# Both attentions of a two-layer block on one core: the loops over batches written out

## The chip, the cores and the metric

The kernel runs on one core of a Trainium2 chip. Five engines take part: TensorE (PE, with its weight loads PEld), VectorE (DVE), ScalarE (ACT), GpSimd (POOL) and SyncE (SP, which here only issues DMAs). The metric is the device time of one execution in microseconds (us).

## The reference

The input x is 8 batches of 512 tokens of 128 features, float32. Four stages follow each other, and each adds to x:

```python
x = x + attn_a(layernorm(x))   # 16 heads of 8, q and k normalised to length 1, softmax(g * q.k)
x = x + ffn(layernorm(x))      # router, top 2 of 8 experts, at most 384 tokens per expert
x = x + attn_b(layernorm(x))   # 16 heads of 64, position bias, softmax, output projection
x = x + ffn(layernorm(x))      # the same weights of the experts again
```

## The kernel before

Five blocks run one after the other: a short setup, attention a (about 20 to 500 us of the profile), the experts, attention b (about 610 to 1680 us), the experts again. In each block every engine has its own program, and the engines meet through semaphores that only count up. A step waits for a count that grows with the batch: `wait(eng, signal, b, k)` (L71) waits for `base + b * per + k`.

In both attentions a batch is software-pipelined into the next one: while batch b is worked on, its successor is normalised and projected, and the router's steps of its predecessor are done. Batch 0 has no predecessor and batch 7 no successor, so these two are written out in Python with constants. Batches 1 to 6 are one loop of the hardware on each engine, in which b is a register: the body stands once in the program, each wait whose count depends on b is computed in registers (`REGISTER_ALU` in the order of instructions), addresses in x_res are computed too, and each of the engines ends the body with its own compare-and-branch. No engine waits for the others at the end of a body. There are five jumps back for six passes, on each engine, in each attention.

What the steps of the prediction name:

- Attention a, per batch 32 chunks: PE makes scores (L836) in one of two PSUM buffers, ACT makes exponentials (L620), PE multiplies them with v (L850), DVE takes the sum over (`take`, L714) and normalises it (`finish`, L719 to L726). DVE's chain of small steps for the lengths of q and k is L660 to L682. At chunk 31 PE makes the router's counts (L301, L303), which wait for DVE (L256). PE's branch is at L899.
- Attention b, per batch 16 steps: PE makes scores (L1232), DVE adds the bias and takes the minimum (`lowest`, L1422), ACT makes exponentials (L1351), PE turns them (L1243), ACT and DVE copy the turned half each (L1343, L1430), PE multiplies with v (L1257), DVE scales (`finish`, L1443, which writes ctxT). At the last step PE makes the output projection (L1267) and DVE adds it to x (`residual`, L1448). DVE's branch is at L1507, ACT's at L1387, PE's at L1310.
- Below, "the seam" of a batch in attention b is the place right after the residual of the batch before it, which is also where DVE's loop jumps back.

The Python condition in attention a's `prepare` on PE (`if not isinstance(b, int) or b > 2`) and the two forms of the operands at stage 0 on DVE depend on whether b is a register.

Of the kernel before, what the change touches and what calls it, by code (L numbers as in the profile page):

```python
# [21 lines left out]
B, S, D = 8, 512, 128  # L22
# [40 lines left out]
def prime(eng):  # L63

    while Signal.made:
        eng.sem_inc(Signal.made.pop().sem, Signal.BASE)


def wait(eng, signal, b, k):

    eng.wait_ge(signal.sem, signal.at(b, k))  # L71
# [327 lines left out]
def attention_a(nc, g, sem):  # L399
# [5 lines left out]
    with ctx:  # L405
# [76 lines left out]
        @block.sync  # L482
        def _(sp):
            prime(sp)
            for n, name in enumerate(("a_Wq", "a_Wk", "a_Wv")):
                sp.dma_start(w_raw[:, n, :], g[name]).then_inc(w_in, 16)
            sp.dma_start(gs[:, :], g["g_scale"].to_broadcast([P, 1])).then_inc(gs_in, 16)
            sp.wait_ge(clear_a, 3)

            def parts_to_dram(b):  # L490

                wait(sp, lo_ready, b, 1)
                for n in range(3):
                    sp.dma_start(k_dram[n].rearrange("d h t -> h d t"), parts[:, n, 1, :]).then_inc(parts_out.sem, 16)
                for n in range(5):
                    sp.dma_start(q_dram[n].rearrange("d h t -> h d t"), parts[:, n % 3, 0, :]).then_inc(parts_out.sem, 16)
                wait(sp, parts_out, b, 16 * 8)
                sp.sem_inc(g["passed_sp"], 1)

            def stacks(grp):  # L500

                r, heads = 3 * DA, slice(4 * grp, 4 * grp + 4)
                for m in range(3):
                    sp.dma_start(k_stack[m * r:(m + 1) * r, heads, :],
                                 k_dram[:, :, heads, :].rearrange("n d h t -> (n d) h t")).then_inc(stacks_in[grp].sem, 16)
                    sp.dma_start(q_stack[m * r:(m + 1) * r, heads, :],
                                 q_dram[m:m + 3, :, heads, :].rearrange("n d h t -> (n d) h t")).then_inc(stacks_in[grp].sem, 16)

            def clears(b):

                sp.dma_start(g["bias_skew"][:, bass.ds(b * (P // B), P // B), :],
                             g["rows"][:, :].unsqueeze(1).to_broadcast([HEADS, P // B, REL])).then_inc(cleared, 16)
                blank(1, b, cleared)

            def blank(f, n, done):
                sp.dma_start(g["slots"][f][bass.ds(n * CAP, CAP), :].rearrange("(p r) w -> p (r w)", p=P),
                             g["blank"][:, :, :].rearrange("p r w -> p (r w)")).then_inc(done, 16)

            def store_x(b):
                wait(sp, res_done, b, GROUPS)  # L520
                sp.sem_inc(g["passed_sp"], 1)
                sp.dma_start(g["x_mid"].rearrange("(b t p) d -> b p t d", b=B, p=P)[bass.ds(b, 1), :, :, :].rearrange("o p t d -> (o p) t d"),
                             x_res[:, bass.ds(b * TB, TB), :]).then_inc(x_stored, 16)

            def batch(b, before):
                for grp in range(GROUPS):
                    wait(sp, stacks_in[grp], b, 16 * 6)
                    sp.sem_inc(g["passed_sp"], 1)
                if before:
                    store_x(b - 1)  # L530
                parts_to_dram(b + 1)
                for grp in range(GROUPS):
                    wait(sp, s_ready, b, 8 * grp + 8)
                    stacks(grp)
                clears(b)

            r.load(sp)
            parts_to_dram(0)
            for grp in range(GROUPS):
                stacks(grp)  # L540
            batch(0, False)
            for n in range(B):
                blank(0, n, slots_clear)
            with sp.Fori(1, B - 1) as b:
                batch(b, True)
            clears(B - 1)
            store_x(B - 2)
            store_x(B - 1)
            sp.wait_ge(cleared, 16 * 2 * B)
            sp.wait_ge(x_stored, 16 * B)  # L550

        @block.gpsimd
        def _(pool):
            nc.gpsimd.memset(q_stack[64:P, :, :], 0.0).then_inc(clear_a, 1)
            nc.gpsimd.memset(k_stack[64:P, :, :], 0.0).then_inc(clear_a, 1)
            pool.wait_ge(clear_a, 2)
            nc.gpsimd.memset(v_ext[:, :, :, :], 0.0).then_inc(clear_a, 1)
            pool.wait_ge(clear_a, 3)
            nc.gpsimd.memset(v_ext[:, :, :, DA:DA + 1], 1.0).then_inc(clear_a, 1)
            pool.wait_ge(clear_a, 4)  # L560

            
            def move_v(grp):
                heads = slice(4 * grp, 4 * grp + 4)
                nc.gpsimd.tensor_copy(v_ext[:, :, heads, 0:DA], v_stage[:, :, heads, :]).then_inc(v_ready.sem, 1)

            def inverse_std(lo, hi, n):
                pool.wait_ge(ln_var, n)
                nc.gpsimd.tensor_tensor(rstd[:, lo:hi], var[:, lo:hi], g["neg_half"][:, 0:hi - lo],
                                        ALU.pow).then_inc(ln_rstd, 1)  # L570

            def batch(b, before):
                if before:
                    r.inverse_std(pool, b - 1)
                wait(pool, v_staged, b + 1, 1)
                for grp in range(GROUPS):
                    wait(pool, av_done, b, 2 * grp + 2)
                    pool.sem_inc(g["passed_pool"], 1)
                    move_v(grp)
                    if before and grp == 0:  # L580
                        r.copy_rows(pool, b - 1)
                if before:
                    r.scatter(pool, b - 1)

            inverse_std(0, TB, 1)
            r.constants(pool)
            wait(pool, v_staged, 0, 1)
            for grp in range(GROUPS):
                move_v(grp)
            inverse_std(TB, NT, 2)  # L590
            batch(0, False)
            pool.wait_ge(slots_clear, 16 * B)
            with pool.Fori(1, B - 1) as b:
                batch(b, True)
            for b in (B - 2, B - 1):
                r.inverse_std(pool, b)
                r.copy_rows(pool, b)
                r.scatter(pool, b)

        @block.scalar  # L600
        def _(act):
# [24 lines left out]

            square(0)
            attend(0, False, True)
            with act.Fori(1, B - 1) as b:
                attend(b, True, True)  # L630
            attend(B - 1, True, False)
            r.exps(act, B - 1)
# [2 lines left out]
        def _(dve):  # L635
# [136 lines left out]
            dve.wait_ge(r.const, 4)  # L772
            dve.wait_ge(ln_rstd, 2)
            batch(0, False, True)
            with dve.Fori(1, B - 1) as b:
                batch(b, True, True)
            batch(B - 1, True, False)
            take(B - 1, 3)
# [11 lines left out]
        def _(pe):  # L790
# [105 lines left out]
                prepare(0, stage)  # L896
            pe.wait_ge(r.w_in, 16)
            attend(0, False, True)
            with pe.Fori(1, B - 1) as b:  # L899
                attend(b, True, True)  # L900
            attend(B - 1, True, False)
            for n in range(2):
# [133 lines left out]
def attention_b(nc, g, sem):  # L1036
    ctx = ExitStack()
    with ctx:
# [84 lines left out]
        def _(sp):  # L1123
# [34 lines left out]

            inverse_rows(0, 0)
            batch(0, False, True)  # L1160
            with sp.Fori(1, B - 1) as b:
                batch(b, True, True)
            batch(B - 1, True, False)
            store_x(B - 1)
# [2 lines left out]
        @block.gpsimd  # L1167
        def _(pool):
            for n in two:
                nc.gpsimd.memset(inv_pad[n][:, :], 0.0).then_inc(pad_clear, 1)  # L1170
            def batch(b, before, more):
                if before:
                    r.inverse_std(pool, b - 1)
                    r.copy_rows(pool, b - 1)
                    r.scatter(pool, b - 1)
                if more:
                    norm_pool(nc, pool, g, ln, lnb, b + 1)

            norm_pool(nc, pool, g, ln, lnb, 0)
            r.constants(pool)  # L1180
            batch(0, False, True)
            with pool.Fori(1, B - 1) as b:
                batch(b, True, True)
            batch(B - 1, True, False)
            r.inverse_std(pool, B - 1)
            r.copy_rows(pool, B - 1)
            r.scatter(pool, B - 1)

        @block.tensor
        def _(pe):  # L1190
# [116 lines left out]

            for d in range(LEAD, LAST):
                step(0, d, d >= FIRST)
            with pe.Fori(1, B - 1) as b:  # L1310
                for d in range(FIRST, LAST):
                    step(b, d, True, b - 1)
            for d in range(FIRST, LAST):
# [6 lines left out]
        def _(act):  # L1320
# [63 lines left out]

            for d in range(LEAD, LAST):
                step(0, d, d >= FIRST)
            with act.Fori(1, B - 1) as b:  # L1387
                for d in range(FIRST, LAST):
                    step(b, d, True, b - 1)
            for d in range(FIRST, LAST):  # L1390
# [4 lines left out]
        def _(dve):  # L1395
# [108 lines left out]
            dve.wait_ge(x_in[1], 16)  # L1504
            for d in range(FIRST, LAST):
                step(0, d, True)
            with dve.Fori(1, B - 1) as b:  # L1507
                for d in range(FIRST, LAST):
                    step(b, d, True, b - 1)
            for d in range(FIRST, LAST):  # L1510
# [84 lines left out]
```

## Time and profile before

| | us |
|---|---|
| three executions | 1774.84 median, 1772.44 to 1777.78 |
| the profiled execution | 1776.62 |
| its span, first to last instruction | 1774.9 |
| share of the span: PE, ACT, DVE, POOL busy | 81%, 53%, 50%, 15% |
| instructions in the profile | 27286 |

The profile shows, for a core's engines, when each instruction ran and, where an engine sat idle before one, what released it. An instruction of a register, a wait or a branch is not counted as busy. "issue" as the releaser means that the engine waited for nothing that the profile shows. A row of the timeline gives start, duration, engine, line, operation and, in brackets, the idle time before it and its releaser. A row of windows gives a stretch, its length, the busy time of PE, PEld, DVE, ACT and POOL with the number of instructions (of DVE alone where it says so), the granted TensorE clock (1.00 is 2.4 GHz, 0.50 would be 1.2 GHz throughout), the DMA share and GB/s.

### The profile page before, as it was taken

The page shows a single profiled execution, that of the slowest core. Times are in us where ns is not written, and L with a number is a line of the kernel's source. Part 1 is how long each engine was busy: PE and PEld are TensorE (multiplying, and loading weights), DVE is VectorE, ACT ScalarE, POOL GpSimd, SP SyncE. Part 2 cuts the span into 40 slices and gives each one's busy share as a digit, 9 for nine tenths or more (in the row PEclk, how much of TensorE's full clock was granted, in tenths as well). Part 3 has the DMA queues.
Part 4 walks back from the last instruction along what each step waited for, and adds up shares of the span by engine and source line. Part 5 has one row for each costly group of instructions (what it writes and reads, how often), then busy time and mean ns, then how long its engine had stood idle before and what let it go on. Part 6 is the DMA issues. An engine that isn't in the chain of part 4 may idle for free. (4 is left out here: it accounts for less than half of the span.)

```text
span 1774.9 us, 27286 instructions
## 1 busy us (share of the span) xinstructions
PE 1444.2 (81%) x7697; PEld 718.2 (40%) x7735; DVE 889.2 (50%) x2700; ACT 936.4 (53%) x1844; POOL 269.3 (15%) x277
## 2 busy tenths in 40 slices
PE   2388788877629089999999998998998998999464
PEld 1122222222217034454454454554544544544343
DVE  2445545444311036657656666557566566566311
ACT  0367666667404047656655655655656565565031
POOL 4101122222124400001001002002002002001135
PEclk9999998999859579999999999999999999999777
DMA  3355444555229300001001000000000000000052
GB/s 67 78 104 134 91 97 89 112 111 110 36 75 287 60 12 19 21 17 33 24 14 36 19 24 24 18 25 20 19 19 18 19 24 13 18 25 19 13 142 25
DMA packets 83135, 93.73 MB, mean 53 GB/s; under 512 B 19934, under 2 KB 60845, under 8 KB 83024
## 3 DMA queue, kind: packets, MB, share of 16 engines
q1 hardware_dynamic: 72016, 86.21, 19.5%
q0 software_dynamic: 11008, 6.39, 2.6%
q14 instruction: 84, 0.69, 0.1%
q8 instruction: 27, 0.44, 0.1%
HBM read 61.75 MB, written 36.09 MB: 55 GB/s over the span
## 5 line engine op out<-in xcount | busy, mean ns | idle before, releaser
L1422 DVE CUSTOM_DVE_ANT_0 biased<-s_ps,bias 128x512 f32<-128x512 f32 x512 | 332.8, 687 | 98.7 <-PE s_ps L1232 60.5
L1351 ACT ACTIVATE probs_b<-biased,low 128x512 f32<-128x512 f32 x512 | 362.7, 711 | 17.3 <-DVE low L1422 17.3
L620 ACT ACTIVATE probs_a<-score_ps,gbound 128x1024 f32<-128x1024 f32 x256 | 269.1, 1114 | 155.3 <-PE score_ps L836 127.0
L1343 ACT ACTIVATE pT<-p_ps 128x512 f32<-128x512 f32 x256 | 152.3, 595 | 323.5 <-PE p_ps L1243 278.5
L1243 PE MATMUL p_ps<-ident,probs_b 128*128 128x128 f32 x2048 | 281.5, 279 | 39.0 <-ACT pT L1343 22.7
L1243 PEld LDWEIGHTS p_ps<-ident,probs_b 128*128 128x128 f32 x2048 | 229.9, 142 | 203.8 <-issue 124.7
L1232 PE MATMUL s_ps<-kT,qT 64*128 64x512 f32 x1024 | 264.5, 635 | 1.4 <-ACT kT L1337 1.4
L1257 PE MATMUL o_psb<-pT,v_b 128*64 128x512 f32 x1024 | 233.8, 598 | 0.0
L1430 DVE COPY pT<-p_ps 128x512 f32<-128x512 f32 x256 | 176.3, 689 | 54.2 <-PE p_ps L1243 49.5
L836 PE MATMUL score_ps<-q_stack,k_stack 128*128 128x512 bf16 x474 | 140.1, 401 | 58.1 <-ACT probs_a L620 30.0
L330 POOL DMA_INDIRECT slots<-rows_r,slot_r x128 | 126.1, 985 | 363.9 <-DVE slot_r L279 324.6
L1232 PEld LDWEIGHTS s_ps<-kT,qT 64*128 64x128 f32 x1024 | 89.9, 192 | 138.2 <-issue 106.3
L1443 DVE TENSOR_TENSOR ctxT<-o_psb,inv_row 128x512 f32<-128x512 f32 x64 | 44.3, 692 | 198.9 <-PE o_psb L1257 194.5
L850 PE MATMUL o_ps<-probs_a,v_ext 128*32 128x512 f32 x1024 | 142.3, 630 | 0.0
L1257 PEld LDWEIGHTS o_psb<-pT,v_b 128*64 128x64 f32 x1024 | 67.8, 136 | 157.0 <-issue 155.9
L316 POOL TENSOR_TENSOR ln_r_r<-ln_vareps_r,neg_half 128x4 f32<-128x4 f32 x16 | 16.5, 1034 | 593.9 <-DVE ln_vareps_r L212 540.9
L836 PEld LDWEIGHTS score_ps<-q_stack,k_stack 128*128 128x128 bf16 x512 | 41.9, 101 | 150.0 <-ACT probs_a L620 97.4
L1351 ACT ACTIVATION_READ_ACCUMULATOR probs_b<-biased,low 128x1 f32 x512 | 97.6, 191 | 0.0
L714 DVE COPY o_sb<-o_ps 128x512 f32<-128x512 f32 x32 | 22.1, 692 | 150.5 <-PE o_ps L850 141.8
L1015 DVE TENSOR_TENSOR o_b_f<-O_f,e_b 128x384 f32<-128x384 f32 x16 | 8.9, 557 | 134.0 <-PE O_f L989 129.0
L1223 PE MATMUL m_ps<-xT_b,wk 128*128 128x512 f32 x128 | 70.8, 635 | 1.7 <-ACT qT L1337 1.7
L1210 PE MATMUL m_ps<-wv,xT_b 128*128 128x512 f32 x128 | 68.5, 618 | 1.5 <-ACT v_b L1331 0.8
(148 smaller groups left out, 1338.1 us busy)
## 6 DMA issues: line engine op xcount, KB each, us to landing
inv_row<-inv_rows SPq DMA_DIRECT2D x128, 128.0 KB
k_stack<-k_parts SPq DMA_DIRECT2D x96, 96.0 KB
q_stack<-q_parts SPq DMA_DIRECT2D x96, 96.0 KB
bias_skew<-bias_rows SPq DMA_DIRECT2D x8, 1024.0 KB
w_f<-in_w SPq DMA_DIRECT2D x32, 256.0 KB, 5.5
bias<-bias_skew SPq DMA_DIRECT2D x16, 448.0 KB
q_parts<-parts SPq DMA_DIRECT2D x40, 128.0 KB, 2.4
inv_rows<-inv_turned SPq DMA_DIRECT2D x256, 1.0 KB
```

Source lines behind the costliest of these rows:

```text
L330: self.nc.gpsimd.indirect_dma_start(self.g["slots"][self.f], bass.IndirectOffsetOnAxis(ap=self.slot[:, k, t:t + 1], axis=0), self.rows[:, ...
L620: nc.scalar.activation(probs[q % 2][:, c % 4, :], score_ps[c % 2][:, :], ACT.Exp, bias=gbound[:, :]).then_inc(p_ready.sem, 1)
L836: last = nc.tensor.matmul(score_ps[c % 2][:, n * S:(n + 1) * S], k_stack[:, head, kt * P:(kt + 1) * P], q_stack[:, head, :], start=True, s ...
L850: last = nc.tensor.matmul(o_ps[hh * VW:(hh + 1) * VW, :], v_ext[:, half * 2 + n, grp * 4 + hh, :], probs[q % 2][:, hh, n * S:(n + 1) * S], ...
L1223: nc.tensor.matmul(m_ps[:, :], (wq, wk)[part][:, n * P:(n + 1) * P], xT[:, :], start=True, stop=True).then_inc(qk_ps.sem, 1)
L1232: last = nc.tensor.matmul(s_ps[k % 2][s][:, :], qT[n % 2][own(s), i * P:(i + 1) * P], kT[n % 2][own(s), :], start=True, stop=True)
L1243: last = nc.tensor.transpose(p_ps[s][:, i * P:(i + 1) * P], probs[n % 2][:, s, i, kt * P:(kt + 1) * P], g["ident"][:, :])
L1257: last = nc.tensor.matmul(o_ps[own(s), :], v[:, kt, h * DH:(h + 1) * DH], pT[t % TB][s][:, :], start=(kt == 0), stop=(kt == TB - 1), skip_ ...
L1343: nc.scalar.activation(pT[t % TB][0][:, :], p_ps[0][:, :], ACT.Copy).then_inc(pT_ready[0].sem, 1)
L1351: nc.scalar.activation(probs[n % 2][:, s, i, :], biased[k % 2][s][:, :], ACT.Exp, bias=low[n % 2][:, s, i:i + 1], scale=-1.0, accum_out=su ...
L1422: nc.vector.tensor_tensor_reduce(out=biased[k % 2][s][:, :], in0=s_ps[k % 2][s][:, :], in1=bias[:, h, off:off + S], scale=1.0, scalar=3.0e ...
L1430: nc.vector.tensor_copy(pT[t % TB][1][:, :], p_ps[1][:, :]).then_inc(pT_ready[1].sem, 1)
```

## The change

Ten loops of the hardware become Python loops. Each engine's program now holds batches 1 to 6 one after the other, with constants for the counts and addresses, and no branch. The operations on data, their order on each engine, the buffers and the counts waited for stay. One of the ten places, the others alike (SP, POOL, ACT, DVE and PE in attention a; SP, POOL, PE, ACT and DVE in attention b):

```diff
             for d in range(FIRST, LAST):
                 step(0, d, True)
-            with dve.Fori(1, B - 1) as b:
+            for b in range(1, B - 1):
                 for d in range(FIRST, LAST):
                     step(b, d, True, b - 1)
             for d in range(FIRST, LAST):
                 step(B - 1, d, False, B - 2)
```

What DVE's program of attention b held at the end of the loop's body, up to the branch (L1422 is `lowest`, L71 a wait's register arithmetic, L1448 the residual):

```order
L1422 ISA biased,low<-s_ps,bias 128x512 [waits p_ready_b]
L1422 ISA low 128x1
L71 REGISTER_ALU
L1430 COPY pT<-p_ps 128x512 [waits pT_ps,av_done_b]
L1448 ISA [waits y_done_b]
L1448 TENSOR_TENSOR x_res<-x_res,m_ps 128x512
L1507 REGISTER_ALU
L1507 COMPARE_AND_BRANCH
```

and what stands at the same place of batch 1 in the program after the change, with the first rows of batch 2 behind the residual:

```order
L1422 ISA biased,low<-s_ps,bias 128x512 [waits p_ready_b]
L1422 ISA low 128x1
L1430 COPY pT<-p_ps 128x512 [waits pT_ps,av_done_b]
L1448 TENSOR_TENSOR x_res<-x_res,m_ps 128x512 [waits y_done_b]
L1422 ISA biased,low<-s_ps,bias 128x512 [waits p_ready_b,s_ready_b]
L1422 ISA low 128x1
```

The register arithmetic and the branch are gone; the data operations follow each other as before.

On PE at the end of attention a's body (L301 and L303 are the router's counts, L836 the scores) there stood:

```order
L71 REGISTER_ALU
L301 MATMUL aux_ps<-chosen_r,upper 128x32 [waits r_step0]
L303 MATMUL aux_ps<-before_r,ones_sq 128x32
L899 REGISTER_ALU
L899 COMPARE_AND_BRANCH
```

and now, with the first scores of the next batch:

```order
L303 MATMUL aux_ps<-before_r,ones_sq 128x32
L836 MATMUL score_ps<-q_stack,k_stack 128x512 [waits p_ready,stacks_in0]
L836 MATMUL score_ps<-q_stack,k_stack 128x512
L836 MATMUL score_ps<-q_stack,k_stack 128x512 [waits p_ready]
```

The scores stand directly behind the counts. Counted in rows of this order with their repeats, DVE's body of attention b held 407 entries, of which 146 were register arithmetic, and ACT's 263 with 130; attention a's bodies held 156 on DVE and 79 on ACT.

## Rows read from the trace of the kernel before

**Rows 1.** The page's first line.

```profile
span 1774.9 us, 27286 instructions
```

**Rows 2.** Windows: batches 4 and 5 of attention b, seam to seam (us, busy, PEclk).

```profile
1159.25:1288.39 129.14, 123.25 (x646) 64.76 (x646) 80.26 (x241) 76.60 (x186) 10.53 (x11) 0.99 0.07 20
1288.39:1416.20 127.81, 121.85 (x646) 64.02 (x646) 80.18 (x241) 76.60 (x186) 10.55 (x11) 1.00 0.06 19
```

**Rows 3.** Timeline of DVE at a seam inside the loop.

```profile
1159.25 0.69 DVE L1448 TENSOR_TENSOR x_res<-x_res,m_ps 128x512 f32 x1 [5.92 <-PE m_ps L1267]
1162.70 0.69 DVE L1422 CUSTOM_DVE_ANT_0 biased<-s_ps,bias 128x512 f32<-128x512 f32 x1 [2.76 <-issue]
```

**Rows 4.** What is on line L1507, DVE's branch in attention b (ns).

```profile
L1507 DVEq COMPARE_BRANCH  x6: 55/63/74, 900.9 to 1545.3; - x6
```

**Rows 5.** Timeline of DVE behind the seam where the loop is entered, without a jump back.

```profile
774.22 0.69 DVE L1422 CUSTOM_DVE_ANT_0 biased<-s_ps,bias 128x512 f32<-128x512 f32 x1 [0.53 <-PE s_ps L1232]
...
782.21 0.69 DVE L1443 TENSOR_TENSOR ctxT<-o_psb,inv_row 128x512 f32<-128x512 f32 x1 [2.98 <-PE o_psb L1257]
```

**Rows 6.** Windows of DVE: residual to a later ctxT (L1443), batches 1 to 6; 1, 7.

```profile
773.00:782.21 9.21, 5.29 (x15) 1.00 0.01 3
900.83:911.54 10.71, 5.20 (x16) 1.00 0.01 2
1030.21:1040.57 10.36, 5.20 (x15) 1.00 0.01 2
1159.25:1169.82 10.57, 5.20 (x16) 1.00 0.01 2
1288.39:1298.94 10.55, 5.20 (x15) 1.00 0.01 2
1416.20:1426.57 10.37, 5.21 (x16) 1.00 0.01 2
773.00:825.39 52.39, 36.68 (x113) 1.00 0.07 21
1545.25:1598.10 52.85, 36.61 (x113) 1.00 0.08 21
```

**Rows 7.** Timeline of PE at the seam of rows 3.

```profile
1154.80 4.29 PE L1267 MATMUL m_ps<-wo,ctxT 128*128 128x128 f32 x37
...
1164.67 0.66 PE L1243 MATMUL p_ps<-ident,probs_b 128*128 128x128 f32 x4 [1.34 <-DVE pT L1430]
```

**Rows 8.** Timeline of ACT at the same seam.

```profile
1161.63 0.60 ACT L1343 ACTIVATE pT<-p_ps 128x512 f32<-128x512 f32 x1 [7.40 <-PE p_ps L1243]
```

**Rows 9.** Timeline of PE at a batch's end in attention a.

```profile
217.25 0.41 PE L301 MATMUL aux_ps<-chosen_r,upper 128*128 128x32 f32 x2 [0.97 <-DVE before_r L256]
```

**Rows 10.** Timeline of ACT: first exponentials of batches 3 and 7, attention a.

```profile
218.55 1.11 ACT L620 ACTIVATE probs_a<-score_ps,gbound 128x1024 f32<-128x1024 f32 x1 [1.91 <-PE score_ps L836]
...
426.73 1.11 ACT L620 ACTIVATE probs_a<-score_ps,gbound 128x1024 f32<-128x1024 f32 x1 [1.71 <-PE score_ps L836]
```

**Rows 11.** What is on line L899, PE's branch in attention a (ns).

```profile
L899 PEldq COMPARE_BRANCH  x6: 76/215/238, 166.0 to 425.7; - x6
```

**Rows 12.** Windows of DVE: L660 to L682 for batch 1 (constants) and 4 (registers).

```profile
88.37:94.72 6.35, 5.91 (x17) 1.00 0.00 0
240.86:247.21 6.35, 5.91 (x17) 1.00 0.00 0
```

**Rows 13.** Windows: batches 4 and 6 of attention a, first exponentials to the next.

```profile
270.38:324.47 54.09, 44.35 (x249) 15.22 (x252) 26.51 (x85) 34.54 (x35) 10.72 (x14) 0.91 0.47 99
376.19:426.73 50.54, 40.33 (x248) 14.33 (x252) 26.35 (x84) 34.40 (x35) 10.69 (x14) 1.00 0.46 96
```

**Rows 14.** Timeline of ACT in batch 3 of attention a.

```profile
235.43 1.11 ACT L620 ACTIVATE probs_a<-score_ps,gbound 128x1024 f32<-128x1024 f32 x1 [4.89 <-remote]
```

**Rows 15.** The page's DMA queues that carry instructions: packets, MB, share.

```profile
q14 instruction: 84, 0.69, 0.1%
q8 instruction: 27, 0.44, 0.1%
```

More of the change, by code:

```diff
@@ L543, in _ @@
                 blank(0, n, slots_clear)
-            with sp.Fori(1, B - 1) as b:
+            for b in range(1, B - 1):
                 batch(b, True)
@@ L592, in _ @@
             pool.wait_ge(slots_clear, 16 * B)
-            with pool.Fori(1, B - 1) as b:
+            for b in range(1, B - 1):
                 batch(b, True)
@@ L628, in _ @@
             attend(0, False, True)
-            with act.Fori(1, B - 1) as b:
+            for b in range(1, B - 1):
                 attend(b, True, True)
@@ L774, in _ @@
             batch(0, False, True)
-            with dve.Fori(1, B - 1) as b:
+            for b in range(1, B - 1):
                 batch(b, True, True)
@@ L898, in _ @@
             attend(0, False, True)
-            with pe.Fori(1, B - 1) as b:
+            for b in range(1, B - 1):
                 attend(b, True, True)
@@ L1160, in _ @@
             batch(0, False, True)
-            with sp.Fori(1, B - 1) as b:
+            for b in range(1, B - 1):
                 batch(b, True, True)
@@ L1181, in _ @@
             batch(0, False, True)
-            with pool.Fori(1, B - 1) as b:
+            for b in range(1, B - 1):
                 batch(b, True, True)
@@ L1309, in _ @@
                 step(0, d, d >= FIRST)
-            with pe.Fori(1, B - 1) as b:
+            for b in range(1, B - 1):
                 for d in range(FIRST, LAST):
@@ L1386, in _ @@
                 step(0, d, d >= FIRST)
-            with act.Fori(1, B - 1) as b:
+            for b in range(1, B - 1):
                 for d in range(FIRST, LAST):
@@ L1506, in _ @@
                 step(0, d, True)
-            with dve.Fori(1, B - 1) as b:
+            for b in range(1, B - 1):
                 for d in range(FIRST, LAST):
```

## The prediction

> **What bounds the kernel now.** I looked for the seams between batches first, because the change acts there and on the register arithmetic inside a batch, and nowhere else. The windows of whole batches give attention b's rhythm: 129.14 us for a batch, in which PE is busy 123.25 and DVE 80.26 [rows 2]. So PE sets attention b's pace, and a delay on another engine counts only as far as PE comes to wait for it. Then the timeline at the seam: behind the residual DVE stands idle for 2.76 us although no semaphore holds it ("issue") [rows 3]. The branch itself takes 63 ns by its record [rows 4]; what follows it takes the time. Where the loop is entered without a jump back, the same `lowest` starts after 0.53 us and its wait is for PE [rows 5]. PE has meanwhile begun the next scores, and then waits 1.34 us for DVE's copy of the turned half [rows 7]. That is the stall arriving on the engine that sets the pace.
>
> In attention a the batch takes 50.54 to 54.09 us with PE busy 40 to 44 [rows 13]: PE, ACT and DVE wait for one another in turn, so a latency anywhere in that ring can count.
>
> **The change part by part.**
>
> *DVE's jumps back in attention b.* I measure what one costs to the end of the kernel, not what DVE idles. From the residual to the first ctxT behind it the batch takes 9.21 us in the pass that was entered from above, and 10.71, 10.36, 10.57, 10.55 and 10.37 in the five passes entered by a jump [rows 6]. They sum to 52.56; five times 9.21 is 46.05; the jumps cost 6.51 us together, 1.30 each. The rest of the 2.76 is taken up by slack that DVE has there. With the stall gone, `lowest` waits for PE's scores again, as in [rows 5]. The upper bound of a seam is its whole idle time less that wait, 2.76 - 0.53 = 2.2, so 11 for five; the shift of ctxT is nearer to the time of the batch, since PE's work of that batch follows it, and I take 6.5.
>
> Here a page bears on it. The Trainium skill, "Runtime: NRT & Kernel Launch", section "Instruction fetch mechanics", says that a taken branch whose target isn't in the two pages at hand forces a fetch of the page before execution goes on. The trace agrees: the large body of DVE (407 entries) stalls by microseconds, the small ones of attention a don't. The skill's "Advanced Engine Details and Errata", section "Control Flow Timing", gives about 108 ns for a compare-and-branch; by that alone five jumps would be an estimated 0.5 us and nobody could measure the change. Rows 3 decide for the larger cost.
>
> *ACT's jump in attention b.* Its copy after the seam had stood idle 7.40 us waiting for PE [rows 8], so whatever the jump costs lies in that wait: 0. If the cover were gone it could cost what DVE's does.
>
> *PE's jump in attention b.* It is issued while the output projection of 4.29 us runs [rows 7]: 0.
>
> *PE's jump in attention a.* The counts wait for DVE and start at 217.25 [rows 9]; the scores of the next batch stand behind them and the branch, and ACT waits for these scores: 1.91 us at a jump, and 1.71 where batch 7 is entered and the branch falls through [rows 10]. The branch takes 215 ns in the middle and 76 at least [rows 11], which agrees. Five times 0.20 is 1.0 us. Bounds: 0, if the loading of k and q ends last there after the change, and 5 x 0.24 = 1.2, the longest record.
>
> *Other jumps.* DVE in attention a jumps while waiting for PE's last values, SP while its transfers run, POOL behind its scatter and ahead of work for which nobody is yet waiting. I take 0 for them together. An unhidden jump would be at most PE's 0.24 each time, since none of these short bodies shows an idle stretch like that of rows 3.
>
> *Register arithmetic.* DVE's seventeen small dependent steps are where it should show: 6.35 us with constants, for batch 1, and 6.35 with registers, for batch 4 [rows 12]. It runs ahead of the engine's work. Over a longer stretch I compare pass 1 with batch 7, which was written out already and does the same up to there: 52.39 with registers, 52.85 with constants [rows 6]. So constants gain nothing; I take 0, with 0.46 a batch as the bound on the loss side (6 x 0.46 = 2.8 us). On the gain side ACT's 1.91 against 1.71 is the only such difference, and it is booked above already; I allow the same 0.20 once more per batch in attention a, 1.2 us.
>
> *Fetching more code.* The program's instruction packets on one queue are few, 27 [rows 15], so most of one engine's passes fetched nothing. Now every batch's code comes from memory once. Pass 1 and batch 7 ran code for the first time, at 52.39 and 52.85 us, no slower than the others less their jump. I take 0.
>
> **The sum.** 6.5 + 1.0 = 7.5 us. The profiled execution took 1776.62 us, its span 1774.9 [rows 1], the 1.7 outside it stays. It becomes 1769.1. That execution lies 1.8 above the median of the three, so on the median's scale 1774.84 - 7.5 = 1767.3 us, a gain of 0.42%. A change of less than 0.3% (5.3 us) is about what a measurement of this kernel can't tell from none.
>
> **The rivals.**
>
> *The clock and the ring move.* PE's granted clock was 0.99 in one batch of attention b and 1.00 in the next, and the batches took 129.14 and 127.81 [rows 2]; both had their jump, so 1.3 us a batch hang on whether PE drops to 1.2 GHz for a short while after a pause. In attention a ACT once waits 4.89 us for something that the profile doesn't name [rows 14], and equal batches differ by 3.55 us [rows 13]. The change shifts all phases. Should three batches more or fewer fall into the slow kind in attention b and one in attention a, that is 3 x 1.3 + 3.5 = 7.4: the gain is eaten, 1775 us, or doubled, 1760. For it: this is as large as the spread of the three executions, 5.3 us. Against: five of six passes behave alike, so the pattern is stable. Chance 0.20 towards no change, 0.06 towards a double gain.
>
> *Another wait takes the stall's place.* DVE's stall also lets PE's scores pile up; without it PE may run into ACT's copies or the transfers of the softmax sums. Pass 1 and batch 7 speak against it: their first ctxT still comes early and the lead of 1.4 us is kept to the fourth. If two thirds were given back, 2.2 + 1.0 would remain: 1771.6 us. Chance 0.08.
>
> *Slower: the written-out code comes late.* One mechanism: an engine that reaches code not yet fetched waits as DVE did behind its branch, 2.76 us, of which 1.3 reach the end. Before, the small bodies of attention a and PE's body of attention b were kept; now they are fetched anew each batch, in attention a beside transfers that keep the DMA engines 46% busy [rows 13]. Two late pieces a batch in twelve batches are 24 x 1.3 = 31 us, less 7.5: 1798 us. It decides from 6 late pieces on (no gain), and from 10 on it is slower by more than 0.3%. Against it stand the first passes above. Chance 0.08.
>
> That the change does nothing at all is excluded by the order: the branches are gone.
>
> **How the numbers follow.** Forecast 0.58, of its own range 1763 to 1770; moved phases 0.20 against me and 0.06 for me; stall replaced 0.08; late code 0.08. The predicted time is the forecast's. The range from 1761 to 1775 takes in the forecast with its bounds (gain 7.5 + 1.2 + 1.3 for a batch without the slow clock, or 7.5 - 2.8) and the moved phases, and leaves out late code and the far end of a double gain, some 0.15. Faster by over 0.3%: the forecast except its lower tenth (0.52), the double gain (0.06) and a part of the moved phases (0.09), 0.67. Within 0.3%: what is left of those and the replaced stall, 0.24. Slower: 0.09.
>
> **What would show each step.** In the changed kernel's profile: at all seven seams of attention b the first `lowest` follows the residual after a wait for PE of about 0.5 us and no "issue" of 2 us or more; residual to ctxT is 9.2 to 9.3 us in every batch; a batch is 127.8 us, or 126.5 where the clock stays up; ACT's wait at the start of batches 2 to 6 of attention a is 1.71 instead of 1.91; the chain L660 to L682 stays at 6.35; the instruction packets rise in number without an idle stretch at "issue" beside them. The prediction is wrong if ctxT comes early but the batch is as long as before, if batches of attention a move by more than their seams, or if new idle stretches of 2 to 3 us at "issue" appear inside a batch.

## The result, and the profile after

The changed kernel takes 1758.28 us (median of 7 runs, 1757.22 to 1772.67); the kernel before, beside it, 1772.44 (7 runs, 1770.03 to 1777.78). The ratio is 0.993, with an interval of 0.991 to 0.9951: 12.4 us less by the ratio, 14.2 between the medians. The forecast was a gain of 7.5, to 1767.3 us, with a range from 1761. The direction is right, the size too small, and the time lies below the range.

The profiled execution happens to be the slowest of the seven, 1772.67 us, so I read its seams, not its total. First the page's own lines, which answer to [rows 1, 15]:

```profile
span 1771.0 us, 23821 instructions
...
q8 instruction: 63, 1.03, 0.2%
q14 instruction: 58, 0.48, 0.1%
```

There are 3465 fewer instructions, no branch, and 1.51 MB of instruction packets where there were 1.13. Then DVE's timeline at the same seam as [rows 3]:

```profile
1156.02 0.69 DVE L1448 TENSOR_TENSOR x_res<-x_res,m_ps 128x512 f32<-128x512 f32 x1 [6.01 <-PE m_ps L1267]
1157.23 0.69 DVE L1422 CUSTOM_DVE_ANT_0 biased<-s_ps,bias 128x512 f32<-128x512 f32 x1 [0.52 <-PE s_ps L1232]
```

The idle 2.76 us at "issue" are gone, and `lowest` waits 0.52 us for PE, as it did at the entry [rows 5]. DVE's windows from the residual to the ctxT behind it, answering to [rows 6] (the first is batch 1, the last three are batches 4 to 6):

```profile
773.28:782.65 9.37, 5.29 (x15) 1.00 0.00 0
...
1156.02:1165.40 9.38, 5.29 (x16) 1.00 0.00 1
1284.89:1294.27 9.38, 5.29 (x16) 1.00 0.00 0
1412.55:1422.09 9.54, 5.29 (x15) 1.00 0.00 1
```

10.36 to 10.71 became 9.37 to 9.54. The five middle passes add up to 47.05 us where they had 52.56, so 1.10 a seam (0.83 to 1.33 each), a little under the 1.30 of the forecast, and the entry case itself went from 9.21 to 9.37. Whole batches 4 to 6 of attention b, against [rows 2]:

```profile
1156.02:1284.89 128.87, 124.89 (x646) 65.55 (x647) 80.43 (x242) 76.75 (x186) 10.54 (x11) 0.97 0.07 20
1284.89:1412.55 127.66, 123.64 (x646) 65.28 (x647) 80.42 (x242) 76.75 (x186) 10.51 (x11) 0.99 0.07 20
1412.55:1538.80 126.25, 122.21 (x646) 64.13 (x646) 80.14 (x241) 76.63 (x186) 10.51 (x11) 1.00 0.07 20
```

Identical work takes 126.25 or 128.87 us, beside a granted clock of 1.00 or 0.97. DVE's chain of L660 to L682 takes 6.36 us in batch 3 (6.35 in [rows 12]). The seams account for 5.5 us of a measured 12.4. The profiled execution can't show the rest: its stretch of attention a, from the first exponential of batch 0 to that of batch 7, takes 355.0 us, no less than the 354.2 before. So I took the change apart.

### The profile page after: what moved, and what is told of

It reads as the page before. It is cut to its first block and busy times, and to the rows that moved or that the text cites. A ratio compares the mean times of both kernels' runs of the same rounds, so it can differ in the third digit from the quotient of the medians.

```text
span 1771.0 us, 23821 instructions
## 1 busy us (share of the span) xinstructions
PE 1463.2 (83%) x7735; PEld 722.8 (41%) x7735; DVE 888.3 (50%) x2700; ACT 937.3 (53%) x1844; POOL 269.1 (15%) x277
## 5 line engine op out<-in xcount | busy, mean ns | idle before, releaser
L1422 DVE CUSTOM_DVE_ANT_0 biased<-s_ps,bias 128x512 f32<-128x512 f32 x512 | 332.6, 688 | 74.9 <-PE s_ps L1232 54.9
L1343 ACT ACTIVATE pT<-p_ps 128x512 f32<-128x512 f32 x256 | 152.1, 594 | 325.6 <-PE p_ps L1243 288.4
L836 PE MATMUL score_ps<-q_stack,k_stack 128*128 128x512 bf16 x512 | 151.5, 409 | 47.3 <-ACT probs_a L620 24.0
L330 POOL DMA_INDIRECT slots<-rows_r,slot_r x128 | 125.9, 983 | 364.1 <-DVE slot_r L279 326.3
L850 PE MATMUL o_ps<-probs_a,v_ext 128*32 128x512 f32 x1024 | 146.9, 649 | 0.0
L1443 DVE TENSOR_TENSOR ctxT<-o_psb,inv_row 128x512 f32<-128x512 f32 x64 | 44.3, 692 | 200.4 <-PE o_psb L1257 197.4
L836 PEld LDWEIGHTS score_ps<-q_stack,k_stack 128*128 128x128 bf16 x512 | 43.3, 102 | 148.6 <-ACT probs_a L620 89.5
```

The costliest lines, as they stand in the source:

```text
L330: self.nc.gpsimd.indirect_dma_start(self.g["slots"][self.f], bass.IndirectOffsetOnAxis(ap=self.slot[:, k, t:t + 1], axis=0), self.rows[:, ...
L836: last = nc.tensor.matmul(score_ps[c % 2][:, n * S:(n + 1) * S], k_stack[:, head, kt * P:(kt + 1) * P], q_stack[:, head, :], start=True, s ...
L850: last = nc.tensor.matmul(o_ps[hh * VW:(hh + 1) * VW, :], v_ext[:, half * 2 + n, grp * 4 + hh, :], probs[q % 2][:, hh, n * S:(n + 1) * S], ...
L1343: nc.scalar.activation(pT[t % TB][0][:, :], p_ps[0][:, :], ACT.Copy).then_inc(pT_ready[0].sem, 1)
L1422: nc.vector.tensor_tensor_reduce(out=biased[k % 2][s][:, :], in0=s_ps[k % 2][s][:, :], in1=bias[:, h, off:off + S], scale=1.0, scalar=3.0e ...
```

## The experiments

All ratios are against the kernel before on the same chip. "Us gained" is one less the ratio, times that kernel's median. Four chips came up. I call them A (runs r1 to r8), B (r13 to r16), C (r9 to r12) and D (r17, r18), and this turned out to matter. The chip of the first comparison is not on record; its time and its traces are of the kind of A and B. Which core of a chip ran is not on record either, so "chip" below may mean core.

### Halves of the change, on chip A

The edit is the diff of the change at a subset of its ten lines. `r3` for example:

```diff
-            with pe.Fori(1, B - 1) as b:      # L899, and the four others of attention a
+            for b in range(1, B - 1):
```

> The changed kernel once more, for its spread and for a second trace. Two theories of the gain. Seams: DVE no longer stands still after its jump back in attention b, worth 6.5 us, and PE's jump in attention a is worth 1.0; then the gain is 7 to 8 us here, and what the first comparison showed above that is spread. Ring: something in attention a gains as well, some 5 us more; then the gain is 11 to 14 us again.

> The five loops of attention b alone are written out; attention a keeps its loops. Seams: a gain of 6.5 us (ratio 0.9963), the residual followed by the next minimum after 0.5 us of waiting for PE. Ring: the same here, since its share lies in attention a.

> The five loops of attention a alone are written out; attention b keeps its loops. Seams: a gain of 1.0 us, not to be told from none. Ring: a gain of 5 to 7 us, and some batches of attention a of 46 to 48 us instead of 51 to 54.

> One loop alone is written out: DVE's in attention b. Seams: the same 6.5 us as with all five of attention b, since the jumps of ACT, PE, SP and POOL lie behind other work. If register arithmetic or the other engines' jumps matter, it gains less than all five by more than 1 us.

| run | written out | median us (runs) | ratio, interval | gained |
|---|---|---|---|---|
| before | none | 1774.99 (23) | | |
| r1 | all ten | 1763.88 (6) | 0.9939, 0.9915 to 0.9962 | 10.8 |
| r2 | attention b | 1768.04 (9) | 0.9958, 0.9942 to 0.9974 | 7.5 |
| r3 | attention a | 1768.29 (12) | 0.9971, 0.9954 to 0.9988 | 5.1 |
| r4 | DVE in attention b | 1769.87 (9) | 0.9963, 0.9948 to 0.9979 | 6.6 |

DVE's loop of attention b is worth 6.6 us by itself, and the other four loops there add nothing that can be told from zero. That term of the forecast stands. Attention a is worth 5.1, where the forecast had 1.0. In the windows of ACT's first exponentials, batch 2 of attention a shows where much of it lies; first the kernel before, then r1 with batch 3 behind it:

```profile
167.20:218.55 51.35, 41.59 (x249) 14.62 (x252) 26.49 (x85) 34.51 (x35) 10.86 (x14) 0.97 0.51 107
```

```profile
164.59:211.83 47.24, 41.01 (x253) 14.56 (x252) 26.58 (x86) 34.41 (x35) 10.86 (x14) 1.00 0.55 118
211.83:264.61 52.78, 43.75 (x253) 15.25 (x252) 26.63 (x85) 34.40 (x35) 10.69 (x14) 0.94 0.50 104
```

The same code takes 47.24 us in one batch and 52.78 in the next. A cheaper wait or branch would take the same from every batch, so this is something else. The timeline of r1 in batch 3 shows it, ACT first, then PE, then POOL:

```profile
220.89 2.12 ACT L620 ACTIVATE probs_a<-score_ps,gbound 128x1024 f32<-128x1024 f32 x2 [1.23 <-PE score_ps L836]
228.05 2.12 ACT L620 ACTIVATE probs_a<-score_ps,gbound 128x1024 f32<-128x1024 f32 x2 [5.04 <-remote]
```

```profile
223.64 1.03 PE L836 MATMUL score_ps<-q_stack,k_stack 128*128 128x512 bf16 x4
224.60 1.07 PE L850 MATMUL o_ps<-probs_a,v_ext 128*32 128x512 f32 x8
229.22 0.61 PE L836 MATMUL score_ps<-q_stack,k_stack 128*128 128x512 bf16 x2 [3.56 <-ACT probs_a L620]
```

```profile
216.67 1.06 POOL L330 DMA_INDIRECT slots<-rows_r,slot_r  x1 [0.57 <-issue]
...
225.71 0.97 POOL L330 DMA_INDIRECT slots<-rows_r,slot_r  x1 [0.30 <-issue]
```

PE has issued the scores of chunks 8 and 9 by 224.67 and goes on to other products, but ACT, which needs the scores, starts at 228.05. In the trace's semaphore events the two increments of `s_ready` for these chunks come at 228.03 and 228.07. An undisturbed pair is 0.43 us apart (254.78 and 255.21). So the increments come some 3 us late and bunched. It happens while POOL issues the router's eight indirect DMAs (L330, one each 1.28 us from 216.67 on; the six between the two rows shown are left out), and it ends 1.4 us after the last. This is the unnamed wait of [rows 14]. The profile calls the releaser "remote", because no event that it knows fits.

The wait is not one of attention a alone. ACT's table of waits for the kernel before (us in total, times, longest) has it in both attentions, L1343 being attention b's copy of the turned half:

```profile
ACT pT L1343 <- remote: 43.2, 7, 6.2
...
ACT probs_a L620 <- remote: 28.2, 11, 4.9
```

In attention b it comes once in each batch from batch 1 on, 6.1 to 6.2 us long, beside the router's eight DMAs (POOL issues them from 835.0 to 845.1 us, the first of these waits ends at 846.64). Written out it is named four to seven times, and the stretch from the first to the last residual doesn't follow the count: 880.3 us with four (r1), 879.9 with seven (r14). So nothing of attention b's gain can be put down to it.

### The indirect DMAs left out, and single engines, on chip A

r5 and r6 leave out the scatter of the router's rows in attention a (and POOL's wait on its landing), so the first experts read blank rows. Attention b keeps its scatter. r7 and r8 are the kernel before with one loop written out.

```diff
     def scatter(self, pool, b):
...
-        for k in range(TOPK):
+        if self.f == 1:
+            for k in range(TOPK):
...
```

> Leaves out the eight indirect DMAs per batch with which the router of attention a scatters its rows (L328 to L332 for the first router, and the wait on them), so the first slots keep their blank rows; all loops stay. The trace of before has ACTIVATE waits of 3 to 5 us once in each of batches 2 to 6 of attention a (4.89 us at 235.43, [rows 14]) that end 1.3 to 1.8 us after POOL's last indirect DMA. If these DMAs cause the wait, the stretch from batch 0's first exponential to batch 7's, 354.2 us in before's profile, loses about 3 us in each of six batches: 332 to 340 us, and the kernel's time is 12 to 20 us below before's. If the wait has another cause and only happens to lie there, the stretch stays at 350 or more and the kernel's time moves by less than 4 us.

> Same omission, with attention a's five loops written out. Theory S (stall): the gain of about 5 us of written-out attention a comes from a different length of the wait beside the scatter; with the scatter gone this kernel and the one with loops differ by under 1.5 us. Theory W (waits): it comes from the cost of waits whose values are computed in registers, on every chunk (ACTIVATE's idle before c=4 is 1.83 us with loops and 1.58 written out), which the scatter has nothing to do with; then this kernel is 3.5 to 6.5 us below the one with loops, and all six middle batches are shorter by 0.6 to 1.1 us each.

> Only TensorE's loop of attention a (L899) is written out. If the gain of attention a lies in TensorE's register waits and its jumps, nearly all of the 5 us is here: 1768 to 1771 us where before has 1773 to 1775. If it lies in ScalarE's, or in the SP and POOL loops, this one gains under 1.5 us.

> Only ScalarE's loop of attention a (L629) is written out. ScalarE is the engine that waits for TensorE before each chunk of probabilities, and TensorE for it; a register computed before each wait adds some 0.06 to 0.09 us ahead of the ACTIVATE at every fourth chunk, 8 a batch, over six batches 3 to 4 us if all of it shows. If that is the term: 2.5 to 4.5 us below before. If the register work is hidden because the wait's release comes later than the register's value: under 1 us.

| run | what | median us (runs) | ratio, interval | gained |
|---|---|---|---|---|
| before | | 1773.54 (23) | | |
| r5 | no scatter in a, loops | 1709.07 (5) | 0.9641, 0.9627 to 0.9655 | 63.7 |
| r6 | the same, a written out | 1708.70 (5) | 0.9635, 0.9621 to 0.9648 | 64.7 |
| r7 | PE's loop of a written out | 1776.79 (12) | 1.0016, 1.0004 to 1.0029 | -2.8 |
| r8 | ACT's loop of a written out | 1770.53 (11) | 0.9982, 0.9970 to 0.9994 | 3.2 |

Two batches of attention a in r5, windows:

```profile
211.77:258.34 46.57, 40.86 (x254) 14.54 (x252) 26.49 (x85) 34.40 (x34) 2.80 (x6) 1.00 0.50 106
258.34:304.91 46.57, 40.87 (x254) 14.55 (x252) 26.51 (x85) 34.40 (x35) 2.80 (x6) 1.00 0.50 105
```

Without the indirect DMAs the middle batches take 46.57 us each, to the hundredth, where the loops had 50.5 to 54.1. None of attention a's waits is left, while attention b, which keeps its DMAs, keeps its seven (42.4 us in all). On this chip the wait goes with these DMAs: that is shown. Whether their issue, their transfer or their landing does it is not. The stretch from the first exponential of batch 0 to that of batch 7 falls from 354.17 to 325.46 us. The other 35 us of r5 are behind it: the last batch's router no longer waits for the rows before it to land, nor the experts for the last ones. From batch 7's first exponential to the experts' first matmul it is 66.2 us, where the kernel before has 98.5 (and r12, on a chip without the wait, 99.6). So these 35 are the price of an order of work and not of the wait. I had not expected that part, and 12 to 20 was my figure for the whole.

r6 against r5 decides between my two theories on this chip. With the DMAs gone, written-out code is worth 1.0 us by the ratios and 0.4 between the medians, which can't be told from nothing, and not the 3.5 to 6.5 of theory W: theory S. PE's loop alone (r7), where the forecast's 1.0 us sat, costs 2.8, which a jump saved gives no reason for; that a moved phase does it is argued only. ACT's loop alone (r8) gains 3.2, inside the 2.5 to 4.5 that I had given for register work ahead of ACT's waits. But such a price would be there without the DMAs too, and r6 here and r18 below don't have it.

### The scatter moved, split, and the rest of the loops, on chip C

```diff
-                    r.scatter(pool, b - 1)
+                    wait(pool, p_ready, b + 1, 6)     # r9 (loops), r10 (a written out)
+                    r.scatter(pool, b - 1)
```

```diff
         for k in range(TOPK):
+            if k == 1:                                # r11, all written out
+                wait(pool, self.scattered, b, 16 * TB)
             for t in range(TB):
```

> All loops stay; the router's eight indirect DMAs of attention a are issued only when ScalarE has done chunk 5 of the batch (a wait of POOL on p_ready ahead of r.scatter in its batch), some 3 us later than now, in six batches. Theory P (phase): how long TensorE's increments are held depends on which matmuls fall beside these DMAs, so that a shift of 3 us changes attention a by several us in either sign (by over 3 us), and the added time of the chunks moves from chunks 5 to 7 to later ones. Theory C (constant): the DMAs cost about 5 us a batch wherever they lie; then the time stays within 3 us of before, unless the rows come free too late and VectorE waits for them, which would show as a longer chunk 11 to 16.

> The same shift with attention a's loops written out. If the 4 us that written-out attention a gains beyond the 1 us it gains without the DMAs is a matter of phase (theory P), then with both kernels tied to the same chunk their difference shrinks to that of the kernels without the DMAs, 0 to 2 us. If the difference stays at 4 to 6 us, the written-out code shortens the wait itself whatever its phase.

> The changed kernel, with the eight indirect DMAs issued four by four: POOL waits for the first four rows' landing before it issues the fifth, in both attentions. In the trace of the changed kernel TensorE's increments come late only from about the fifth DMA on. If what holds them is the number of indirect DMAs issued and not yet carried out, the waits of 3 to 5 us get shorter or vanish: 5 to 25 us below the changed kernel's 1764. If it is the issuing itself, the time stays within 4 us of it or rises, since rows come free some 2 us later.

> Only VectorE's, POOL's and SP's loops of attention a are written out (L775, L593, L544). TensorE's alone gave +2.8 us and ScalarE's alone -3.2, all five -5.1. If the parts add, this one is 4 to 6 us below before. If they don't (phase), it may come out anywhere from -3 to +3 us.

| run | median us (runs) | ratio, interval | gained |
|---|---|---|---|
| before | 1725.09 (29) | | |
| r9 | 1725.40 (11) | 1.0002, 0.9993 to 1.0011 | -0.3 |
| r10 | 1725.12 (12) | 1.0000, 0.9991 to 1.0008 | 0.0 |
| r11 | 1742.94 (4) | 1.0104, 1.0089 to 1.0118 | -17.9 |
| r12 | 1724.73 (11) | 0.9994, 0.9985 to 1.0003 | 1.0 |

The surprise is in the first line. The unchanged kernel takes 1725.09 us on this chip, 48 less than on chip A, in 29 runs between 1722.86 and 1728.91. r12's windows of attention a (its six middle batches are still loops on PE and ACT) show why:

```profile
210.92:257.48 46.56, 40.20 (x249) 14.55 (x252) 26.71 (x85) 34.41 (x34) 10.66 (x14) 1.00 0.56 119
257.48:304.04 46.56, 40.20 (x249) 14.55 (x252) 26.58 (x85) 34.41 (x35) 10.66 (x14) 1.00 0.53 114
```

That is r5's batch with the indirect DMAs in it (POOL busy 10.66). Chip C issues them and has no wait: the DMAs are needed for it, but they are not enough. In ACT's table of waits, "remote" is the mark. On chip B, with the loops (r13), the rows are these; on C (r12) and D (r17) there is none, in either attention:

```profile
ACT pT L1343 <- remote: 43.1, 7, 6.2
...
ACT probs_a L620 <- remote: 29.6, 12, 4.6
```

So r9 and r10 could not test the phase: there was nothing whose phase to move. They show only that issuing the scatter later is free there (4.2 us later in r9's trace against r12's, where I had meant 3). r12 could not show either whether the parts of the gain add up. r11 meant to shorten the wait and had none to shorten; what it shows is its own cost. Each half waits for its landing. Against r12 on the same chip the first residual of attention b comes 9 us later (753.8 against 744.8), and attention b's batches take 125.8 to 128.3 us where r12 has 124.4 to 125.9, jumps and all, so that the last residual is 16.7 us later. No better version came of it. A scatter cut in two was not tried on a chip with the wait.

### The change again, on chips B and D

Kernels as in the first group; r13 is the kernel before.

> The kernel before, unchanged, for its profile on the chip of this call. On a chip without the late increments: about 1725 us, attention a's middle batches 46.56 us each; on one with them: about 1774 us, batches of 49 to 54 us.

> All ten loops written out. Theory S (the extra gain of attention a belongs to the wait beside the indirect DMAs): on a chip without the wait the change gains 6.5 us for VectorE's jumps in attention b and about 1 for attention a, 1716.5 to 1719 us where the kernel before has 1725. Theory W (the written-out code itself is faster in attention a): 10 to 12 us below before, 1713 to 1715. On a chip with the wait: 1762 to 1766, as measured before.

> Only attention a written out. Theory S on a chip without the wait: 0 to 2.5 us below before, and batches of 46.1 us where the loops have 46.56. Theory W: 4 to 6 us below. On a chip with the wait: 5 us below.

> Only attention b written out. By the forecast's term of 1.30 us for each of VectorE's five jumps: 5.5 to 7.5 us below before on either kind of chip. If attention b's gain too was a matter of the wait, under 3 us on a chip without it.

> As for the same kernel before: on a chip without the wait 6 to 8.5 us below the kernel before by theory S, 10 to 12 by theory W; on a chip with it 10 to 12 either way (three times measured: 14.2, 11.1, 9.9).

> On a chip without the wait 0 to 2.5 us below the kernel before by theory S, 4 to 6 by theory W; on a chip with it 4 to 7 (twice measured: 6.7 and 5.3 between medians, 5.1 and 4.1 by the ratios).

| run | chip | written out | median us (runs) | ratio, interval | gained |
|---|---|---|---|---|---|
| before | B | none | 1776.63 (35) | | |
| r13 | B | none | 1777.16 (12) | 0.9999, 0.9981 to 1.0016 | 0.2 |
| r14 | B | all | 1766.77 (12) | 0.9950, 0.9929 to 0.9970 | 8.9 |
| r15 | B | a | 1771.36 (12) | 0.9977, 0.9961 to 0.9992 | 4.1 |
| r16 | B | b | 1771.24 (12) | 0.9970, 0.9952 to 0.9988 | 5.3 |
| before | D | none | 1725.36 (19) | | |
| r17 | D | all | 1719.65 (7) | 0.9970, 0.9959 to 0.9981 | 5.2 |
| r18 | D | a | 1725.18 (12) | 1.0001, 0.9991 to 1.0011 | -0.2 |

Chip B has the wait and repeats chip A. Chip D has none, and there written-out attention a gains nothing that can be measured (-0.2, interval -1.9 to 1.6) while the whole change gains 5.2 us. The time on chip B is just above my 1762 to 1766, and the 5.2 of chip D is under my 6 to 8.5; the interval of the second reaches from 3.3 to 7.1. ACT's timeline of r17 at the place where r1 waited 5.04 us:

```profile
219.95 2.12 ACT L620 ACTIVATE probs_a<-score_ps,gbound 128x1024 f32<-128x1024 f32 x2 [0.83 <-PE score_ps L836]
223.74 2.12 ACT L620 ACTIVATE probs_a<-score_ps,gbound 128x1024 f32<-128x1024 f32 x2 [1.67 <-PE score_ps L836]
```

POOL issues its eight DMAs from 216.13 to 226.13 there, at the same place. Attention b on chip D is the cleanest view of the jump. Two middle batches of r18 (b in loops), then of r17 (written out):

```profile
1121.24:1246.38 125.14, 122.14 (x646) 64.00 (x646) 80.24 (x242) 76.47 (x186) 10.52 (x11) 1.00 0.07 20
1246.38:1371.55 125.17, 122.14 (x646) 64.00 (x646) 80.20 (x242) 76.46 (x186) 10.52 (x11) 1.00 0.06 20
```

```profile
1117.24:1241.39 124.15, 122.47 (x646) 64.04 (x646) 80.22 (x241) 76.72 (x186) 10.49 (x11) 1.00 0.06 21
1241.39:1365.58 124.19, 122.49 (x646) 64.06 (x647) 80.22 (x242) 76.72 (x186) 10.53 (x11) 1.00 0.07 20
```

A middle batch is 0.99 and 0.98 us shorter here, at a clock of 1.00 on both sides, and from the residual to the ctxT behind it, where the jump acts, it is 9.38 us against 10.38. The whole of attention b gives back less in these two profiles: from the first to the last residual 858.9 us against 862.2, since written out batches 1 and 6 are 0.5 and 0.6 us longer.

## Why the forecast was too small

**DVE's jumps in attention b, 1.30 each, 6.5 together: right.** Its loop alone gave 6.6 (r4), all of b 7.5 and 5.3 (r2, r16), and on a chip without the wait 5.5 (r17 less r18). A single seam measures 1.0 there, 1.1 on average in the first trace after. The excess of the old middle passes was counted against the entry pass at 9.21, which is 9.37 in the changed kernel, so 0.16 of each 1.30 was not gained. The timeline came out as the forecast described it, a wait of 0.52 us for PE at all seven seams. The rule of the Trainium skill ("Runtime: NRT & Kernel Launch", "Instruction fetch mechanics"), that a taken branch to a page not at hand waits until it is fetched, agrees in direction: in the trace before, 2.55 to 2.90 us at "issue" stand behind each of the five jumps and none at the two other seams. That a fetch fills this time no run here shows, and the size had to come from the rows.

**ACT's, PE's and the other engines' jumps in attention b, 0: right** within what r2 against r4 can tell (7.5 against 6.6, each known to some 2.8 us).

**Attention a, 1.0 for PE's jump and nothing for the ring of waits: this is the step that failed.** The sum had only the jump, with "register arithmetic" at 0 and the rival "the clock and the ring move" left out as something that might fall either way. On chips with the wait attention a gained 5.1 and 4.1 (r3, r15). On one without it, -0.2 (r18, interval -1.9 to 1.6). The sign that I had named for the 1.0 did not come: ACT's wait at the start of batches 2 to 6, 1.91 to 1.94 us before, is 1.71 in one batch of r17 and 1.85 to 2.80 in the other four. PE's jump alone lost 2.8 (r7). So the 1.0 is not confirmed, though r18's interval does not exclude it, and most of the 4 to 5 us was never part of a jump.

They belong to that rival. I had its row in hand, 4.89 us of ACT waiting for something unnamed [rows 14], and batches that differ by 3.55 us [rows 13], and treated both as noise, which could move a batch either way. I also wrote that ACT waits so once. The trace before has such a wait in each of batches 2 to 6 of attention a, 3.3 to 4.9 us long, and in seven batches of attention b. They are one mechanism, absent in batches 0 and 1, in which no scatter is issued yet. That pattern was in the trace before. Of a fixed stretch of 354 us, 29 were this wait and what followed it: r5 has 325.46. With so much at stake, a rival of 0.06 for a double gain was too small. In middle batches without the wait, written-out code takes 45.7 to 47.0 us where loops take 46.56 (r17 against r12), and the stretch 324.5 against 324.9. With the wait, batch 2 took 47.24 us in r1 against 51.35 before [its window above], and batches 3 to 6 moved little; over the five profiles of loops and the five of written-out code on such chips, batch 2 averages 51.7 and 48.3, and the whole stretch 354.6 and 349.2. So about 3.4 of the 5.4 us are in the first of the batches that the wait reaches. The five written-out ones run from 344.1 to 355.0, so this gain is no steady one.

**Chains of small steps, 0: right** (6.36 against 6.35). **Fetching more code, 0: right**, though I had read one of two queues: the packets of both are 121 where there were 111. No engine has 2 to 3 us at "issue" at a seam any more. My sign against the forecast, such stretches inside a batch, did come: 2.97 us before a ctxT at 841.46 us in the first trace, 4.72 us before an exponential at 336.15. Neither speaks for late code. r17 has the same 2.97 us at the same ctxT (812.01), named as an ordinary wait for PE, so that one is a matter of the name. The other is the wait beside the router's DMAs once more (POOL issues them from 325.5 to 335.5), at chunk 8 as in batches 3, 4 and 6; r17, all written out on a chip without the wait, has none. The rival "slower" didn't come up in any of the profiles.

**The median's scale.** The first result's 12.4 us (8.7 to 16.0 by its interval) are the 5 to 7 of attention b and the 4 to 5 of attention a, at the upper end of both; 10.8 and 8.9 in repetition. On the chips without the wait the forecast of 7.5 is too large, not too small: 5.2.

Two things stay open. Why TensorE's increments come late beside indirect DMAs on two chips and not on two others, no run here says. And why batch 2 is shorter in written-out code: on chip A it escapes the wait (47.2 to 47.5 us), on B only in part (49.6 and 50.2), and r2 has 48.9 with loops. That its matmuls meet the eight DMAs at another phase is argued only, since the runs that were to move the phase came to a chip without the wait.

## What to carry to other kernels

A hardware loop's jump costs what the engine idles behind it less the slack of the pace-setting engine; read it off one event behind the seam, in the passes with and without a jump. Here that gave 1.30 us where 1.0 to 1.1 was measured. Before forecasting a small gain, look for the largest wait with no named releaser, see in which batches it is missing and what they lack. Here it was 29 us of attention a, more than all the jumps together, and some 24 in attention b. A gain that depends on such a wait is a gain only on chips that have it, two of four here; time both kernels on more than one before believing either.

## What the runs showed that I had not expected

- The same program takes 1773.5 to 1776.6 us on two chips and 1725.1 to 1725.4 on two others. From the first exponential of attention a to that of batch 7 it is 354.2 against 324.9 us (before, r12), and from the first to the last residual of attention b in loops 887.8 against 863.7. Each has the wait on one kind of chip and not on the other, and together they differ by 53 us, the two profiles' spans by 51.5.
- While POOL issues a run of indirect DMAs, TensorE's increments can come 3 to 5 us late and bunched, on those two chips. Of ACT's own in that stretch, the trace has those for chunks 4 and 7, and they came on time (chunk 7's at 223.02, 0.01 after the exponential's end).
- Leaving out the eight indirect DMAs per batch of attention a saved 64 us of 1774 there: 29 of the wait, and 35 behind attention a, where router and experts wait for their rows on either kind of chip.
